# Transposed attention scores of the last two sequences, computed by turns in two pairs of PSUM banks

## The reference, cut to what matters

```
q = (hidden_states @ wq.T + bq) * scaling      # 12 heads of 16
k = hidden_states @ wk.T + bk
v = hidden_states @ wv.T + bv
k = p_rope(k, positions); q = p_rope(q, positions)
attn = softmax(einsum('bqd,bkd->bqk', q, k))
out = einsum('bqk,bkd->bqd', attn, v)
return out @ wo.T + bo
```

## Time and profile before

| | |
|---|---|
| median of three runs | 1570.99 us (1569.74 to 1573.64) |
| the profiled execution's own time | 1572.42 us |
| its span in the trace | 1570.2 us |
| TensorE busy | 1494.2 us, 95% of the span |
| VectorE busy | 1347.7 us, 86% |
| ScalarE busy | 1242.8 us, 79% |
| GpSimd busy | 850.5 us, 54% |
| mean granted TensorE clock | 0.979 of full |

### The profile page before, as it was taken

One profiled execution on the slowest core, in us unless ns is written; L12 is line 12 of the kernel. 1 busy time (PEld: TensorE's weight loads), 2 busy tenths in 40 slices (PEclk: granted clock), 3 DMA queues, 4 the chain that ended last, 5 costly groups with the idle time before them and its releaser, 6 DMA issues.

```text
span 1570.2 us, 36660 instructions
## 1 busy us (share of the span) xinstructions
PE 1494.2 (95%) x11441; PEld 1212.6 (77%) x11441; DVE 1347.7 (86%) x3200; ACT 1242.8 (79%) x2686; POOL 850.5 (54%) x1400
## 2 busy tenths in 40 slices
PE   4799999999999999999999997999999999999996
PEld 3678878888888888888888886677777777777763
DVE  5899999999999999999999986688888878888764
ACT  4678879898888888888888864778878777877863
POOL 7888855453335443333333245666666666666642
PEclk9899999999999999999999997999999999999998
DMA  5634201000000000000000000000000000000000
GB/s 113 141 61 83 31 1 34 1 35 0 0 1 1 1 1 0 0 1 1 1 0 0 1 1 2 2 8 12 12 16 11 11 11 11 11 11 16 11 12 26
DMA packets 24445, 27.16 MB, mean 17 GB/s; under 512 B 3104, under 2 KB 22432, under 8 KB 24352
## 3 DMA queue, kind: packets, MB, share of 16 engines
q1 hardware_dynamic: 16672, 19.70, 4.0%
q0 software_dynamic: 7680, 6.30, 3.2%
HBM read 14.58 MB, written 6.29 MB: 13 GB/s over the span
## 4 chain that ended last, share of the span: by engine, by line
PE 69%; POOL 11%; ACT 8%; DVE 6%; issue 6%; DMA 0%; ACTq 0%; DVEq 0%; POOLq 0%
PE banks L723 9%; PE banks L741 7%; PE banks L986 7%; PE banks L732 6%; PE banks L954 6%; POOL x L455 5%; PE banks L911 5%; PE banks L938 5%; PE banks L925 4%; PE banks L846 3%; PE banks L814 2%; PE banks L897 2%; PE banks L1010 2%; PE banks L850 2%; PE banks L900 2%
## 5 line engine op out<-in xcount | busy, mean ns | idle before, releaser
L1691 DVE TENSOR_REDUCE mx<-banks 128x4 f32<-128x1024 f32 x192 | 234.1, 1219 | 45.5 <-PE banks L925 45.1
L1297 ACT ACTIVATE probs<-banks 128x1024 f32<-128x1024 f32 x192 | 195.8, 1020 | 85.4 <-PE banks L938 81.9
L521 POOL TENSOR_TENSOR x<-x,bo_row 128x768 f32<-128x768 f32 (+1 forms) x64 | 120.1, 1876 | 129.0 <-DVE ucr_r L1552 129.0
L723 PE MATMUL banks<-ht,w_uv 128*128 128x512 f32 x576 | 171.2, 407 | 14.2 <-ACT sv_l L1271 12.2
L497 POOL TENSOR_TENSOR lnt<-mv,const 128x4 f32<-128x4 f32 x64 | 27.2, 425 | 267.3 <-DVE mv L1517 267.3
L1543 DVE SCALAR_TENSOR_TENSOR uc_h<-u_h,vec,uc_h 128x512 f32<-128x512 f32 x192 | 154.1, 803 | 2.2 <-ACT uc_h L1204 2.2
L723 PEld LDWEIGHTS banks<-ht,w_uv 128*128 128x128 f32 x576 | 107.2, 194 | 47.8 <-issue 20.9
L723 PE MATMUL banks<-ht,w_uv_rest 128*128 128x512 f32 x384 | 121.4, 398 | 0.0
L938 PE MATMUL banks<-q_t,k_t 64*128 64x256 f32 x768 | 109.3, 336 | 7.4 <-ACT probs L1297 5.9
L1543 DVE SCALAR_TENSOR_TENSOR uc_l<-u_l,vec,uc_l 128x256 f32<-128x256 f32 x192 | 104.1, 542 | 7.8 <-issue 2.9
L1526 DVE SCALAR_TENSOR_TENSOR xs<-x,rstd,xs 128x192 fp32r<-128x192 f32 x256 | 93.6, 425 | 18.3 <-ACT xs L1248 18.3
(11 more groups left out here) (189 smaller groups left out, 4719.3 us busy)
## 6 DMA issues: line engine op xcount, KB each, us to landing
out_dram<-y_out SPq DMA_DIRECT2D x32, 192.0 KB, 2.0
x<-pos SPq DMA_DIRECT2D x12, 384.0 KB, 4.2
raw_z<-w_z_dram SPq DMA_DIRECT2D x4, 704.0 KB, 5.5
raw_uv<-w_uv_dram SPq DMA_DIRECT2D x4, 576.0 KB, 4.0
q_t<-mx_t SPq DMA_DIRECT2D x64, 6.0 KB
emb<-w_qkv_dram SPq DMA_DIRECT2D x1, 864.0 KB, 7.5
w_o<-w_o_dram SPq DMA_DIRECT2D x1, 768.0 KB, 5.2
x<-embedding_dram,idx POOLq DMA_INDIRECT x48, 4.3
```

The lines of the kernel that those rows point to most:

```text
L521: nc.gpsimd.tensor_tensor(rows, rows, bo_row[:, l, :][:, None, :].broadcast_to([P, CT, D]), ALU.add).then_inc(x_biased, 1)
L723: last = nc.tensor.matmul(out[:], w, r[:], start=(k == 0), stop=(k == len(passes) - 1))
L1297: act.activation(probs[:, (s + g // 2) % 2, g % 2, :].rearrange("p (j k) -> p j k", j=2), B_SST, ACT.Exp, scale=float(DH) ** -0.5).then_in ...
L1691: nc.vector.tensor_reduce(mx[:, s].rearrange("p t (j h) -> p j t h", j=2)[:, :, :, g], B_SS.rearrange("p j (t k) -> p j t k", t=2), AX, AL ...
```

## The change

The transposed scores of the sequences at lag 4 in steps 34 and 35 (sequences 30 and 31) go by turns into two pairs: even groups into `B_ST` as before, odd groups into `B_S`. The exponentials of odd groups read `B_S`. A group then waits for the exponentials of the group two before it. Group 1 of step 34, the first in `B_S`, waits for the last of all maxima (`max_done` at 192). All steps before 34, the order of instructions on every engine, their number and their sizes stay.

```
+        def alternating(m):
+            return isinstance(m, int) and m >= SEQ + 2
+        def pair_of(m, g):
+            return g % 2 if alternating(m) else 0
...
-            def scores_t(it, g):
+            def scores_t(m, it, g):
                 if it is None:
                     return
                 n, s = it
                 wait(pe, mt_placed[s], 16 * (n - s) + 32)
-                wait(pe, exp_done, 6 * n + g)
+                if not alternating(m) or m == SEQ + 2 and g == 0:
+                    wait(pe, exp_done, 6 * n + g)
+                elif m == SEQ + 2 and g == 1:
+                    pe.wait_ge(max_done, 6 * SEQ)
+                else:
+                    wait(pe, exp_done, 6 * n + g - 1)
+                pair = (B_ST, B_S)[pair_of(m, g)]
                 for t in range(2):
                     for j in range(2):
                         q = slice(HS * j, HS * j + HS)
-                        last = nc.tensor.matmul(B_ST[j][:, t * S:(t + 1) * S], k_t[q, s, g, t * P:(t + 1) * P],
+                        last = nc.tensor.matmul(pair[j][:, t * S:(t + 1) * S], k_t[q, s, g, t * P:(t + 1) * P],
                                                 q_t[q, s, g, :], start=True, stop=True)
...
-            def exps(it, g):
+            def exps(m, it, g):
...
-                act.activation(probs[:, (s + g // 2) % 2, g % 2, :].rearrange("p (j k) -> p j k", j=2), B_SST, ACT.Exp,
+                act.activation(probs[:, (s + g // 2) % 2, g % 2, :].rearrange("p (j k) -> p j k", j=2),
+                               (B_SST, B_SS)[pair_of(m, g)], ACT.Exp,
                                scale=float(DH) ** -0.5).then_inc(exp_done, 1)
```

More of the change, by code:

```diff
@@ L1101, in step2 @@
                         project_o(at(5))
-                    scores_t(at(4), g)
+                    scores_t(at(None), at(4), g)
                     if g == 5 and last:
@@ L1393, in step2 @@
                         turned(B_OTT, or_t, ott_done, at(5)[0], ott_saved)
-                    exps(at(4), g)
+                    exps(at(None), at(4), g)
                     save_heads(at(2), g)
```

## The result

Over 22 runs of each kernel the median is 1568.48 us with the change and 1574.6 us before; the ratio is 0.9963, with a 95% interval of 0.9952 to 0.9975. That is 5.8 us less, between 3.9 and 7.6. Two of the 22 runs of before, at 1804.59 and 1990.01 us, were slow ones and do not count in the ratio. The prediction was 1565.1 us, 5.85 us under the 1570.99 us of the three runs shown with it. Against the 1570.99 us themselves the changed kernel's median is only 2.5 us lower.

What follows compares the result with a forecast made beforehand. TensorE was taken to bound the kernel, with idle waits and low clock in steps 34 and 35. Waits of 3.1 us plus clock of 2.75 us gave 5.85 us off 1570.99, so 1565.1 us, range 1563.5 to 1568.5.

Steps and rivals of the forecast that it cites:

- The waits: Steps 34 and 35: TensorE no longer idles for the exponentials of the group just before; 3.1 us of the gain.
- its term for the border: Start of step 35: group 0's scores no longer wait for group 5's exponential; 0.12 us.
- The values as the next thing that waits: Steps 34 and 35: with the scores' wait gone, the values wait for ScalarE's exponentials; 0.92 us gained at the first place.
- the unused time of GpSimd: Step 35: GpSimd's factors for the second norm come before VectorE asks for them, with 2 us to spare.
- the price of nothing for the new wait on the maxima: Step 34, group 1: an earlier wait in TensorE's order covers it, so no cost; 0.58 us without that cover.
- The clock: Steps 34 and 35: low-clock stretches behind TensorE's idle places go with them; 1.45 + 1.3 = 2.75 us.
- the rest would move as a whole: Rest of step 35 and steps 36 to 38: same TensorE order, moved earlier together; 20.3 us behind step 35 unchanged.
- The rule: Scores cycling through PSUM banks: the skill page's rule keeps the low-clock stretches, leaving about 3.1 us instead of 5.85.
- The full sum: Steps 34 and 35: waits and low-clock stretches both go, 5.85 us less, 1565.1 us; chance 0.60.
- the rival of the low stretches that stay: Steps 34 and 35: waits go, low clock stays in part or whole; 1567.9 us, or 1566.5 with one stretch; chance 0.25.
- The hidden wait: Steps 34 and 35: values wait for exponentials anyway, so only 1 to 2 us gained, 1569.5 us; chance 0.12.
- the slower case: Steps 34 to 38: new phases keep TensorE's clock low for most of them; 1575.7 us or more; chance 0.03.

Runs made afterwards that it cites:

- the run with pairs by turns: Scores by turns in two pairs of banks as in the change, but with the old waits, against the kernel before: ratio 0.9999, steps 24.22 us.
- The three timed kernels with a part of the change, or its banks alone: Change in step 34 alone, in step 35 alone, or two pairs with the old waits, against the kernel before: ratios 0.9988, 0.9993 and 0.9999.

## Why the prediction was right and where it was wrong

**The waits: right in kind, 3.7 us instead of 3.1.** Against the old waits at full clock, the points of the layout moved thus: group 4's scores of step 34 by 1.03 us (forecast 0.92), the last values of sequence 30 by 1.45 (forecast 1.04 with its term for the border), the first values of sequence 31 by 2.45 (2.02), the values of groups 2 and 3 by 2.91 (2.32), group 5's scores by 3.71 (3.12). Of the 0.6 us that I missed, 0.3 to 0.4 stand at the border of the steps: I let group 0's scores of step 35 start behind the whole feed-forward, and in the timeline after they start at 1536.43, between its matmuls. The values as the next thing that waits, 0.37 us in step 35, the unused time of GpSimd (its factors were ready 1.5 us before VectorE read them in step 35, forecast 2), and the price of nothing for the new wait on the maxima (0.58 us, the same as before) came as forecast.

**The clock: the step that failed.** "Together 5.85 us" counts 2.75 us for low stretches as if they stood in every execution of before and went with the idle places. In the steps the size was right where they stood: 26.90 - 24.22 = 2.68 us, of which 1.47 us lie in step 34 (forecast 1.45) and 1.15 us in step 35 (forecast 1.3, though its parts as given add up to 1.46). But they stood in two of five executions with the old waits in both steps, so they cost 25.33 - 24.22 = 1.1 us on the mean, which the change does save: none of its five executions has one. And the tail of the changed kernel is slower on the mean, 17.59 us against 16.64: 0.95 us. That row of the prediction said the rest would move as a whole; in order it does, its clock does not. Sum over five executions of each: (25.33 + 16.64) - (20.52 + 17.59) = 41.97 - 38.11 = 3.9 us, which is 3.7 us of waits and 0.2 us of clock. (One of the five with the old waits is the run with pairs by turns, whose order of work and time in the steps are those of before; its tail, 18.18 us, is the only slow one of the five. With the four of before alone the sum is 41.86 - 38.11 = 3.75 us, and the tail of the changed kernel is 1.33 us slower.) So that the timed difference meets the 5.85 us is in part luck: the term of the waits was 0.6 us too small, the term of the clock 2.5 us too large, and some 2 us of the timed difference no trace shows.

What stays open: the timed ratio gives 5.8 us, 3.9 to 7.6, and the traces' mean stands at its lower end. It leaves out what lies behind the start of the last feed-forward, which took 3.92 to 4.19 us with the old waits and 3.94 to 5.05 us with the change, 0.5 us more on the mean; with that it is 3.4 us, below the interval. Five and five executions are few for a clock that differs from one to the next, and I can't say whether the tail's 0.95 us is the change's doing or the draw. That seven of ten unfilled tails with two pairs come to their projection at half clock and none of five with one pair speaks for something in the kernels with two pairs; what it would be, no run shows. The three timed kernels with a part of the change, or its banks alone, are each within 0.12% of before and can't settle it either.

**The rule.** The Trainium skill, page "TensorE: Matmul & The Clock Gate", section "A second HAM failure mode: psum-queue depth-cycling", read as a rule for this kernel, would have had the clock go to and fro as the scores cycle through banks. No run here shows that where they do: with the pairs by turns and the old waits the clock was 1.00 in both steps, and in the five executions of the change too. What it says of small idle pieces between groups agrees with the tail, where filling pieces of 0.6 to 1.1 us, and part of one of 2.7, went with a clock of 1.00 instead of 0.55 to 0.79.

**The level and the chances.** 1565.1 us was worked from 1570.99 us, the median of three runs; the 22 runs of before lie 3.6 us higher. The first 240 us of the program differ by up to 7.7 us between executions of the same kernel, more than the whole change is worth. I had looked at a spread of 3.9 us in three runs and still set the level by them. (The chance of faster adds up from its parts to 0.60, not 0.61.) The full sum, which I gave 0.60, is not what the traces show; they lie nearest to the rival of the low stretches that stay, with the difference that they leave the changed steps and stand behind them. The hidden wait and the slower case did not come.

## What to carry to other kernels

A second buffer pays when the wait on the first is what the engine idles for: lay out the new order with measured distances from start to start, and find what waits next, here the values for ScalarE. A low clock in one trace can be a draw and need not belong to the line where it stands; price it by several executions, or take it away in a run that keeps the waits. Where the end of a kernel is a chain with gaps of about a microsecond on TensorE, matmuls nobody needs can shorten it, by 1.75 us on the mean here (17.59 against 15.84). On the tails of before, 16.11 to 16.66 us, there is less to gain, and it was not tried.

## What the runs showed of the hardware

- The same idle places, 1.21 us in step 34 and 1.29 us in step 35, were followed by half clock in some executions and by full clock in others of the same order; a batch of 16 matmuls behind them took 1.92 or 1.07 us.
- With 71 added matmuls in the tail its granted clock was 1.00 in three executions, against 0.55 to 0.79 in five without, and it was 0.3 to 3 us shorter, though each of the idle pieces they filled was under 1.1 us but one.
- The first four matmuls of the last projection took 0.92 us in all five executions with one pair of banks and 1.65 us in seven of ten with two; the cause is open.
- In the trace matmuls on 64 rows of two batches stand between one another: the first scores of step 35 started 0.01 us after a feed-forward matmul that took 0.25 us (1536.42 and 1536.43).
